# A three-layer graph attention network on one core: attention scores as extra columns of the first projection, and four smaller moves between engines

## The reference

```
x1 = relu(x @ W_ah + b_ah)
for l in 0..2:                                   # 3 layers, 4 heads of 192 features
    h   = (x1 @ W_l).reshape(N, 4, 192)
    as, ad = (h * a_src).sum(-1), (h * a_dst).sum(-1)
    e   = leaky_relu(as[src] + ad[dst], 0.2)     # edges, and one self loop per node
    p   = exp(e - segment_max(e, dst))
    out = segment_sum(p / (segment_sum(p, dst) + 1e-16) * h[src], dst)
    xs_l = relu(out + b_l)
y = layernorm(x + relu(concat(xs_0, xs_1, xs_2) @ W_out + b_out))
```

## Time and profile before

| | us |
|---|---|
| median of 3 runs | 964.36 (963.82 to 965.69) |
| the profiled execution | 963.98 |
| its span, first to last instruction | 962.4 |
| granted TensorE clock, mean | 0.999 |
| PE busy | 937.6 |
| DVE busy | 739.8 |
| ACT busy | 366.8 |
| POOL busy | 45.8 |

### The profile page before, as it was taken

One profiled execution on the slowest core, in us unless ns is written; L12 is line 12 of the kernel. 1 busy time (PEld: TensorE's weight loads), 2 busy tenths in 40 slices (PEclk: granted clock), 3 DMA queues, 4 the chain that ended last, 5 costly groups with the idle time before them and its releaser, 6 DMA issues. The chain is left out here.

```text
span 962.4 us, 14549 instructions
## 1 busy us (share of the span) xinstructions
PE 937.6 (97%) x5662; PEld 869.3 (90%) x5662; DVE 739.8 (77%) x1064; ACT 366.8 (38%) x534; POOL 45.8 (5%) x94
## 2 busy tenths in 40 slices
PE   6999999999999999999999999999999999999997
PEld 2677649999999999999999999999999879999996
DVE  6999986999999299989989988988877282243233
ACT  1566322122212245465555555555555450011000
POOL 4600000000000000010010010010010100000000
PEclk9999999999999999999999999999999999999999
DMA  6350722534442822153252362239331263223211
GB/s 181 55 183 19 259 85 91 165 115 143 140 153 89 229 82 82 64 126 79 84 120 62 93 130 58 78 87 375 101 103 60 87 169 129 81 85 113 75 33 32
DMA packets 57692, 108.16 MB, mean 112 GB/s; under 512 B 14012, under 2 KB 41245, under 8 KB 56486
## 3 DMA queue, kind: packets, MB, share of 16 engines
q1 hardware_dynamic: 39188, 66.22, 22.7%
q0 software_dynamic: 5360, 18.77, 8.0%
q10 hardware_dynamic: 13090, 22.44, 7.5%
HBM read 80.34 MB, written 27.08 MB: 112 GB/s over the span
## 5 line engine op out<-in xcount | busy, mean ns | idle before, releaser
L1311 PE MATMUL ps<-R_W 125*125 125x193 f32 x2400 | 397.8, 327 | 5.0 <-ACT R_XIN L722 3.9
L1311 PEld LDWEIGHTS ps<-R_W 125*125 125x125 f32 x2400 | 391.3, 188 | 8.7 <-ACT R_XIN L722 7.6
L707 ACT ACTIVATE R_W<-R_EXP,s 125x1250 f32<-125x1250 f32 x120 | 161.2, 1344 | 162.3 <-PE ps L1311 93.9
L998 DVE SCALAR_TENSOR_TENSOR R_W<-R_W,R_CNT 125x1250 f32<-125x1250 f32 x120 | 174.4, 1453 | 3.9 <-DVE R_EXP L987 2.0
L957 DVE CUSTOM_DVE_ANT_0 R_ROWS<-R_MASK,R_ROWS 125x1250 bf16<-125x1250 bf16 x100 | 138.6, 1453 | 3.2 <-ACTq L660 3.2
L1228 PE MATMUL ps<-Wl_hi,x_hi 128*125 128x384 f32 x360 | 122.1, 339 | 0.0
L1228 PE MATMUL ps<-Wl_hi,x_lo 128*125 128x384 f32 x360 | 121.7, 338 | 0.0
L1228 PE MATMUL ps<-Wl_lo,x_hi 128*125 128x384 f32 x360 | 121.6, 338 | 0.0
L1370 PE MATMUL ps<-Wo_hi,xs_hi 128*125 128x384 f32 (+2 forms) x324 | 109.5, 338 | 0.3 <-PE ps L1360 0.3
L1370 PE MATMUL ps<-Wo_lo,xs_hi 128*125 128x384 f32 (+2 forms) x324 | 109.4, 338 | 0.0
L1370 PE MATMUL ps<-Wo_hi,xs_lo 128*125 128x384 f32 (+2 forms) x324 | 109.2, 337 | 0.0
(11 more groups left out here) (146 smaller groups left out, 854.0 us busy)
## 6 DMA issues: line engine op xcount, KB each, us to landing
xs_dram<-R_XIN POOLq DMA_DIRECT2D x18, 625.0 KB, 9.3
h_dram<-R_HOUT ACTq DMA_DIRECT2D x30, 336.0 KB
R_W<-h_dram SPq DMA_DIRECT2D x12, 840.0 KB
R_ROWS<-as_dram SPq DMA_DIRECT2D x12, 625.0 KB, 4.4
R_EXP<-u_dram SPq DMA_DIRECT2D x6, 1250.0 KB, 6.4
R_X<-u_dram SPq DMA_DIRECT2D x6, 1250.0 KB, 5.8
R_ROWS<-in_W_all SPq DMA_DIRECT2D x18, 384.0 KB, 3.5
Wo_sb<-in_W_out POOLq DMA_DIRECT2D x1, 6912.0 KB, 27.3
```

The costliest lines, as they stand in the source:

```text
L707: nc.scalar.activation(prob[r % PSLOTS], expo[:, r % XSLOTS], ACT.Exp, bias=s02[:, r % NT, ds(2 * p + r // NT, 1)]).then_inc(S["exp_done"], 1)
L998: nc.vector.scalar_tensor_tensor(out=prob[r % PSLOTS], in0=prob[r % PSLOTS], scalar=HUGE, in1=cntT[:, r % NT, 0:N], op0=ALU.min, op1=ALU.m ...
L1311: ins = mm(ps[0:PT, o:o + HW], prob[r % PSLOTS][:, t * PT:(t + 1) * PT], hB[:, q, j], start=(j == 0 and t % 2 == 0), stop=(j == NT - 1), s ...
```

## The change

Five edits. **(a)** `scores` and `scores_turn` go. V (rounded high part by ACT, low part by DVE) becomes columns 384 to 407 of the first half layer's weights (`HS` = 408), so that part 0 of h gives the scores node-major in PSUM. ACT copies them tile by tile to `asad`. A new `scores_turn` at the start of part 1 transposes the 12 as columns back for the store to `as_dram`. Part 0 is reordered: the high terms of tiles 0 and 3, then the low terms; `rest_x1` makes x1's low part by node group instead of by feature block. `w_raw[0]` waits for one more feature block of x1. **(b)** The shifts come in three rounds: heads 0 to 7 (`ROUND_A`), 8 and 9 inside pair 0, 10 and 11 as before. **(c)** The subtraction for the low parts of W goes from DVE to GpSimd. **(d)** Self loops are added once for each PSUM bank of four windows. **(e)** `tile`: of the first two source tiles of a head, the columns of the head's own banks are done first, and then the others.

```
+ROUND_A = 8
+ROUND_B_AT = 5
+HS = HALF + 2 * LH
@@ SP
-                        sp.wait_ge(S["turn_ps"], x1_whole(2))
+                        sp.wait_ge(S["turn_ps"], x1_whole(3))
                         sp.dma_start(w_raw[0], w_half(0)).then_inc(S["w_in"], 16)
-            sp.wait_ge(S["asadT_sb"], len(GROUPS))
-            sp.dma_start(as_dram, asadT[0:LH]).then_inc(S["as_stored"], 16)
+            sp.wait_ge(S["asT_sb"], len(GROUPS))
+            sp.dma_start(as_dram, asT).then_inc(S["as_stored"], 16)
...
+            store_u(1, ROUND_A, DEFER)
             load_pair(PAIRS - 2)
+            store_u(2, DEFER, LH)
@@ POOL
+            for n in range(PARTS):
+                pool.wait_ge(S["w_hi"], n + 1)
+                nc.gpsimd.tensor_tensor(Wl_lo[n][:, :, 0:HALF], w_raw[n], Wl_hi[n][:, :, 0:HALF].bitcast(f32), ALU.subtract
+                                        ).then_inc(S["w_lo"], 1)
@@ ACT
             act.wait_ge(S["v_made"], 2 * HEADS * KT * LAYERS)
-            act.wait_ge(S["asad_ps"], KT)
-            for g, (t0, w) in enumerate(GROUPS):
-                nc.scalar.copy(asadT[:, t0 * PT:(t0 + w) * PT], bank(2 + g)[0:2 * LH, 0:w * PT]).then_inc(S["asadT_sb"], 1)
-            round_w(1)
+            nc.scalar.copy(Wl_hi[0][:, :, HALF:HS], V).then_inc(S["v_hi"], 1)
...
+                    if n == 0:
+                        nc.scalar.copy(asad[:, t], bank(t % 4)[0:PT, HALF:HS]).then_inc(S["asad_sb"], 1)
-                    if t == ROUND_AT and 1 <= n < PARTS - 1:
+                    if t == ROUND_AT and n < PARTS - 1:
                         round_w(n + 1)
+                    if n == 1 and t == 0:
+                        for i, (g, w) in enumerate(GROUPS):
+                            act.wait_ge(S["asT_ps"], i + 1)
+                            nc.scalar.copy(asT[:, g * PT:(g + w) * PT], bank(5 + i)[0:LH, 0:w * PT]).then_inc(S["asT_sb"], 1)
-            def pair(p, last, shifts_here=False):
+            def pair(p, last, nth=None):
                 for r in range(NT, 2 * NT if last else 3 * NT):
                     exp_tile(p, r)
-                    if shifts_here and r == NT:
-                        shifts_out(len(GROUPS), uT2)
+                    if nth is not None and r == NT:
+                        act.wait_ge(S["u_stored"], 16 * (2 * nth - 1))
+                        shifts_out(nth * len(GROUPS), uT2)
@@ DVE
-            rest_w(0)
-            for m in range(KT):
-                dve.wait_ge(S["turn_sb"], x1_whole(m))
-                dve.wait_ge(S["asad_ps"], m + 1)
-                nc.vector.tensor_tensor(x1_lo[:, m], x1T[:, m], x1_hi[:, m].bitcast(f32), ALU.subtract
-                                        ).then_inc(S["x1_lo"], 1)
+            rest_x1(0, 0, 1)
+            dve.wait_ge(S["v_hi"], 1)
+            nc.vector.tensor_tensor(Wl_lo[0][:, :, HALF:HS], V, Wl_hi[0][:, :, HALF:HS].bitcast(f32), ALU.subtract
+                                    ).then_inc(S["v_lo"], 1)
+            rest_x1(0, 1, KT)
             more_counts()
-
-            dve.wait_ge(S["asadT_ps"], 1)
-            link(nc.vector.tensor_copy(asad[:], bank(7)[0:PT, 0:NT * 2 * LH].rearrange("p (t h) -> p t h", t=NT)))
+            rest_x1(1, 0, KT)
+            rest_x1(2, 0, KT)
+
+            dve.wait_ge(S["asad_sb"], NT)
...
-                    if b == NT - 2 and hh % 2 == 0:
-                        rest_w(hh // 2 + 1)
...
+                if hh == ROUND_A - 1:
+                    for w in range(2):
+                        link(nc.vector.memset(u[:, :, w * LH + ROUND_A:(w + 1) * LH], 0.0))
+                    shifts(0, ROUND_A, z)
+                    if late == (0, 0) and r == ROUND_B_AT:
+                        dve.wait_ge(S["uT_ps"], len(GROUPS))
+                        shifts(ROUND_A, DEFER, z)
@@ PE
+                if u % 2 or u == NU - 1:
+                    b0, b1 = BANKS[u // 2]
+                    own = bank(u // 2 % 2)[0:PT, 0:(b1 - b0) * MC].rearrange("p (x j) -> p x j", j=NT)
+                    d0, d1 = b0 * WD, min(b1 * WD, N)
...
-            for k in range(KT):
-                scores(k)
...
+            def hi_terms(t):
+
+                for i in range(2):
+                    if i == 1:
                         pe.wait_ge(S["w_lo"], 1)
+                        pe.wait_ge(S["v_lo"], 1)
+                    for k in range(KT):
+                        h_product(0, t, k, i, False)
...
+                    hi_terms(0)
+                    hi_terms(3)
+                    lo_terms(0).then_inc(S["h_ps"], 1)
+                    more_counts()
...
+                if j == 0:
+                    pe.wait_ge(S["out_evac"], NT * (2 * p + q) + 1)
+                    if q == 1:
+                        pe.wait_ge(S["attT_sb"], 9 * p + 1)
+                if j < 2:
+                    columns(p, q, j, range(4, NT))
+                if j == 1:
+                    for t in (0, 2):
                         pe.wait_ge(S["out_evac"], NT * (2 * p + q) + t + 3)
+                        ins = columns(p, q, 0, (t, t + 1))
+                    ins.then_inc(S["p_used"], 1)
+                if j >= 1:
+                    columns(p, q, j, OWN_FIRST if j > 1 else range(4)).then_inc(S["p_used"], 1)
...
+                    if nth == 1 and r == NT - 2:
+                        shifts(2)
```

More of the change, by code:

```diff
@@ L632, in round_w @@
                 act.wait_ge(S["w_in"], 16 * n + 16)
-                nc.scalar.copy(Wl_hi[n][:], w_raw[n]).then_inc(S["w_hi"], 1)
+                nc.scalar.copy(Wl_hi[n][:, :, 0:HALF], w_raw[n]).then_inc(S["w_hi"], 1)
             for i in range(x1_upto(NU - 1) // KT + 1, len(X1_ORDER)):
@@ L761, in _ @@
                 exp_tile(0, r)
-            with act.Fori(0, PAIRS - 2) as p:
+            pair(0, False, nth=1)
+            with act.Fori(1, PAIRS - 2) as p:
                 pair(p, False)
-            pair(PAIRS - 2, False, shifts_here=True)
+            pair(PAIRS - 2, False, nth=2)
             pair(PAIRS - 1, True)
@@ L1215, in _, with h_product @@
             pe.wait_ge(S["mask_ready"], 2 * NT)
-            pe.wait_ge(S["v_made"], 2 * HEADS * KT * LAYERS)
-            for k in range(KT):
-                scores(k)
+            TERMS = ((x1_hi, Wl_hi), (x1_hi, Wl_lo), (x1_lo, Wl_hi))
+            def h_product(n, t, k, i, last):
+                xx, ww = TERMS[i]
+                return mm(bank((2 * (n % 2) + t) % 4)[0:PT, 0:HS if n == 0 else HALF], xx[:, k, t * PT:(t + 1) * PT], ww[n][:, k],
+                          start=(k == 0 and i == 0), stop=last, skip_group_check=True)
@@ L1220, in h_products @@
             def h_products(n, t, blocks):
-                place = bank((2 * (n % 2) + t) % 4)[0:PT, 0:HALF]
                 for k in blocks:
-                    if n == 0 and t == 0:
-                        pe.wait_ge(S["x1_lo"], k + 1)
-                        pe.wait_ge(S["w_lo"], 1)
-                    for i, (xx, ww) in enumerate(((x1_hi, Wl_hi), (x1_hi, Wl_lo), (x1_lo, Wl_hi))):
-                        ins = mm(place, xx[:, k, t * PT:(t + 1) * PT], ww[n][:, k],
-                                 start=(k == 0 and i == 0), stop=(k == blocks[-1] and i == 2), skip_group_check=True)
+                    for i in range(3):
+                        ins = h_product(n, t, k, i, k == blocks[-1] and i == 2)
@@ L1267, in h_part @@
                 pe.wait_ge(S["w_hi"], n + 1)
-                if n > 0:
-                    pe.wait_ge(S["w_lo"], n + 1)
-                for t in range(NT):
-                    pe.wait_ge(S["h_sb"], NT * n + t + 1)
-                    first = {1: KT - 1, 2: KT - 2}.get(t, 0) if n == 0 else 0
-                    h_products(n, t, range(first, KT)).then_inc(S["h_ps"], 1)
-                    if n == 0 and t == 0:
+                if n == 0:
+                    pe.wait_ge(S["v_hi"], 1)
+                    hi_terms(0)
+                    hi_terms(3)
+                    lo_terms(0).then_inc(S["h_ps"], 1)
+                    more_counts()
+                else:
+                    pe.wait_ge(S["w_lo"], n + 1)
+                for t in range(1 if n == 0 else 0, NT):
+                    if n > 0 or t > 3:
+                        pe.wait_ge(S["h_sb"], NT * n + t + 1)
+                    if n == 0 and t < 3:
+                        ins = h_products(n, t, range(KT - t, KT))
+                    elif n == 0:
+                        if t > 3:
+                            hi_terms(t)
+                        ins = lo_terms(t)
+                    else:
+                        ins = h_products(n, t, range(KT))
+                    ins.then_inc(S["h_ps"], 1)
+                    if n == 1 and t == 0:
                         scores_turn()
-                        more_counts()
                     if t == U_AT and n == PARTS - 1:
@@ L1294, in _, with columns @@
             pe.sem_inc(S["attT_ps"], 1)
+            def columns(p, q, j, ts):
+                for t in ts:
+                    o = out_at(q, t)
```

(18 more changed lines are left out.)

94 lines of the change are left out of this document (42 added, 52 removed).

## The result

The changed kernel takes 989.65 us (988.95 to 990.11) against 964.6 beside it: ratio 1.0254, 95% interval 1.0243 to 1.0265. Forecast was 951.5, with a range up to 966. Its span is 988.0 us at a mean granted clock of 0.977.

The account below looks back on a forecast made before the run. PE's own stream was taken to bound the kernel. 963.98 - 8.0 (scores as columns) - 6.5 (own columns first) + 1.6 (third round) = 951.1, 951.5 us as a median; own range 947 to 956, for all 946 to 966.

Parts of the forecast that it names:

- I take nothing, by the nearest rows.: V and maxima: GpSimd's subtractions cost DVE 0, with 5.2 us each kept for the range.
- The two casts: Evidence for no hold: a one-input cast took 1.25 us with a GpSimd SBUF read beneath it, the other 1.23.
- The sign that the prediction named for this: Forecast wrong if maxima beside GpSimd's rows are 4 to 7 us apart and PE stands 5 to 20 ahead of attention.
- The second rival: V and maxima: GpSimd keeps DVE out for its T us, five times, 5T - 4.2; 973.3 us at T = 5.2; chance 0.18.
- the way from there to the loaded shifts ends before the last maximum.: Ahead of attention: from PE's tile 2 of h's last part to loaded shifts takes 10.6 us, done before the maxima end.
- (a), PE's arrival: Scores as columns: h starts at 131.3 us, PE reaches attention at 331.6 instead of 339.56, -8.0 us.
- the 4 us of lead: Attention's first weight tile: DVE ready at h + 196.1 us, PE there at h + 200.3.
- the 1.4 us that PE was to wait in `more_counts`: Part 0 of h: DVE ready 8.1 us after V, PE there after 6.7, so +1.4 us.
- (c) as relief for DVE: Maxima of 1.386 us each with no subtraction between; DVE stays ahead of PE only if GpSimd leaves it alone.
- (d), "0 more": Self loops per bank: both engines reach V's seam some 2 us sooner, but the load for V's block 13 eats it.
- (e), "-6.5 us": Attention, own columns first: PE's weight-load stalls at head changes go, -6.5 us, bounds -7.6 and -3.
- The third round, "+1.6 us": Shifts in three rounds: 10 more PE transposes, 1.2 us, and ACT held in pair 0, +0.4.

Follow-up runs that it names:

- a_memset_sp: Changed kernel with loads for heads 10 and 11 behind the first shifts in SP's queue, GpSimd zero-filling W's low parts instead of subtracting (result incomplete): 952.21 us.
- a_sp_early: Changed kernel with only SP's order edited, the first shifts' store and loads ahead of the score loads for heads 10 and 11: 978.79 us.
- a_dve_sp: Changed kernel with the subtractions back on DVE and score loads for heads 10 and 11 behind the first shifts in SP's queue: 966.95 us.
- b_cols_loops: Kernel before the change, with only self loops once per PSUM bank and a head's own columns first: 955.88 us.
- c_load_late: b_cols_loops with the load of `w_raw[0]` waiting for one more feature block of x1, as in the change: 960.17 us.
- b_pool_low: Kernel before the change, with only the subtractions for W's low parts moved from DVE to GpSimd: 981.68 us.
- c_fill2: a_dve_sp with extra PE transposes in its idle stretches, 40 ahead of h and 80 right behind h's last product: 963.74 us.

## Why the prediction was wrong, step by step

The miss is 989.65 - 951.5 = 38.2 us. The runs split 37.4 of it: SP's order 989.65 - 978.79 = 10.9, and GpSimd's reads 978.79 - 952.21 = 26.6. What is left, 0.7 us, is all the rest of the sum together, in which larger misses cancel (a_memset_sp).

**The first step that failed: "I take nothing, by the nearest rows."** GpSimd's subtraction was priced at nothing; it costs DVE nearly its whole duration, 4.9 us of 5.06. The two casts it was judged by the earlier trace rows read one input; every V reduction and every maximum reads two. The sign that the prediction named for this came: maxima beside GpSimd's rows 6.35 us apart (194.74 to 201.09), and PE idle for 19.59 us ahead of attention. The second rival had the right mechanism and wrote its price as 5T - 4.2. T measured 4.9 (maxima: 19.6 / 4), so 5T is 24.5. The 4.2 of slack was not there: in a_memset_sp, where nothing holds DVE, PE still waits 0.77 us for DVE's first weight tile. So the rival's own formula without the slack gives 24.5 of the 26.6. In the profiled executions, a_sp_early against a_memset_sp: h starts 4.0 us later (135.47, 131.43), the first maximum 5.3 (188.38, 183.11), the first exponent 25.1 (348.54, 323.40), and the end is 27.1 later (977.4, 950.3). What is added outside V and the maxima, 1.3 and 2.0 us, lies where PE has just been idle and runs at a lower clock (0.72 from 136 to 140 us, 0.77 from 356 to 365, against 1.00). That the clock is the cause of it is worked out, not run alone in this pair. The Trainium skill, "SBUF — State Buffer", section "Who interferes with whom", says that a two-input DVE instruction contends with a GpSimd instruction that reads SBUF and not with one that only writes it. The three GpSimd forms here agree in all: subtraction 4.9, copy 1.9, fill 0. By that rule the forecast would have been 973.3, on the right side, and still 16 us short, 10.9 of them SP's. The Trainium skill's "GPSIMD Engine Reference", "Performance versus the Vector engine", gives 4.497 us for 2048 elements, which makes 5.06 for 2304, an estimate; the undisturbed subtraction in the trace took 5.06.

**The second: "the way from there to the loaded shifts ends before the last maximum."** DVE's and PE's part of it did: shifts at 321.5, transposes done by 324. The store did not go out, because the prediction did not follow SP's queue past `load_as(10)` and `load_as(11)`. In the kernel before, these stand ahead of the store too and cost nothing, as the shifts there come after all maxima anyway. Splitting the shifts made the order matter. a_sp_early shows it: 10.9 us.

**(a), PE's arrival.** Without the hold (a_memset_sp) h starts at 131.43; 131.3 was predicted. The 24 columns cost what was said, 0.185 us apart. The first maximum comes 51.7 us after h's start, and 49.7 was predicted: the store of the scores takes 3.6 us (173.47 to 177.04 in a_memset_sp), not 2.03. DVE has its first tile 197.7 us after h's start (predicted 196.1), and PE is there after 197.5 (predicted 200.3): of the 4 us of lead, 1.6 went to a later DVE and 2.8 to an earlier PE: the 1.4 us that PE was to wait in `more_counts` did not come.

**(c) as relief for DVE.** The need was seen rightly: (a) starts the maxima late, and DVE can't do the subtractions as well. With them on DVE (a_dve_sp) the kernel is 14.7 us slower than where no engine holds or does them (a_memset_sp), and 13.8 of these are there when attention starts (343.51, 329.69). So a_dve_sp is 11.1 us above b_cols_loops, though its PE does no scores: 5.4 us ahead of attention (343.51, 338.08), 5.3 behind. The late load of `w_raw[0]` cost 4.3 in c_load_late; what it costs here, and the split of the rest, was not run.

**(d), "0 more".** Right for the end of V: without the hold it comes at 130.85 us, and 130.8 was predicted. The late load costs V 2.7 us in c_load_late (130.97, 128.30), near the 3 that the prediction has in it. What the prediction left out is the clock, which brought the cost of the late load from 2.7 to 4.3 us there.

**(e), "-6.5 us".** -6.2 measured. In the changed kernel the stalls at heads 1 and 2 stay (3.5 us), at all other heads they go.

**The third round, "+1.6 us".** Too small. From attention's start to the end a_memset_sp takes 620.6 us and b_cols_loops, with (e) alone in that stretch, 616.4: 4.2 us. The stalls at heads 1 and 2 are in it; it was not split further.

**The clock.** The sum had no term for it. An idle stretch of PE cost 1.3 to 2.9 us more than itself wherever the clock fell behind it and rows price it: 1.7 in c_load_late, 2.9 in b_pool_low, 1.3 and 2.0 above, and 3.2 for two together in c_fill2.

The fastest version run that leaves nothing out is the kernel before with (d) and (e), 955.9 us, or 955.6 with the load one place later: 0.99 of the time before. The scores as columns and the third round did not pay in any version that was run with the subtractions in it. The scores as columns alone, without the late load and the third round, were not run.

## What to carry to other kernels

In these traces work given to GpSimd was free for DVE where it read nothing from SBUF (the fill) or where DVE was idle meanwhile. Beside DVE instructions of two SBUF inputs, count its whole duration on DVE. Beside instructions of one input no run here tested a long one. When a step is moved earlier, read every in-order queue that it passes through, DMA queues too, and ask of each entry ahead of it what it waits for. And price an idle stretch of PE with the slower matmuls behind it.

## What the hardware showed that was not expected

A copy by GpSimd of 2304 elements takes 2.11 us with one input where the subtraction takes 5.06 with two, and holds DVE 1.9. The hold works both ways: GpSimd's copy stretched to 2.76 to 3.35 us and the subtraction to 6.33 beside maxima. And behind similar idle stretches the clock differed: it stayed at 1.00 behind 3.30 us in a_memset_sp, and fell behind 3.20 us in c_load_late. Windows on PE after the idle stretch (us from the start of the span, length, busy, granted clock, DMA share, GB/s), first a_memset_sp:

```profile
133.00:135.00 2.00, 2.00 (x12) 1.00 0.05 12
```

and c_load_late:

```profile
133.00:135.00 2.00, 2.00 (x5) 0.50 0.01 2
```

What tells them apart stays open.
